# Cutting VectorE's long steps of an attention-and-experts block into pieces with places of their own

## The reference

```python
x = x + layernorm(attention(layernorm(x)))
x = x + layernorm(experts(layernorm(x)))
# attention: 16 heads of 16 channels, rotary q and k, causal, softmax, W_o
Q, K, V = (split_heads(layernorm(x) @ W.T) for W in (W_q, W_k, W_v)); Q, K = rope(Q), rope(K)
out = softmax(where(causal, -inf, Q @ K.T / 4)) @ V @ W_o.T
# experts: 16 of 128 hidden channels, 4 chosen for each token, and a shared one of 256
scores = sigmoid(h @ gate_w.T); groups of 4, the best 2 of 4 groups, then the best 4 experts of these
y = sum over chosen e of w_e * (silu(h @ Wg[e].T) * (h @ Wu[e].T)) @ Wd[e].T
y = y + (silu(h @ Ws_g.T) * (h @ Ws_u.T)) @ Ws_d.T ;  return h + y      # all float32
```

## Time and profile before

| | |
|---|---|
| Time, median of 3 runs | 1130.15 us (1129.67 to 1133.27) |
| The profiled execution's own time | 1136.02 us |
| Its span | 1134.2 us |
| TensorE busy | 886.7 us (78%) |
| VectorE busy | 679.0 us (60%) |
| ScalarE, GpSimd busy | 448.6 us (40%), 440.0 us (39%) |
| Mean granted TensorE clock | 0.844 of 2.4 GHz |

### The profile page before, as it was taken

The page is one execution under the profiler, slowest core; times in us unless marked ns, Lnnn a source line. Parts: engine busy times, 40 slices in busy tenths (PEclk is TensorE's granted clock), DMA queues, the critical chain, the costliest instruction groups (busy, mean ns, idle before and its releaser), DMA issues.

```text
span 1134.2 us, 21559 instructions
## 1 busy us (share of the span) xinstructions
PE 886.7 (78%) x7044; PEld 651.4 (57%) x7044; DVE 679.0 (60%) x1918; ACT 448.6 (40%) x756; POOL 440.0 (39%) x422
## 2 busy tenths in 40 slices
PE   4369798887987997888886798695987699988810
PEld 3245465664654665655564555584875588877700
DVE  4467658677668578577476475552652233677737
ACT  2115444444343444443442445342542355444400
POOL 4422113125316316306313114454555545555642
PEclk9659898897798698798696789898998999988955
DMA  3684716217226235324465322343544555987764
GB/s 131 149 228 106 215 39 168 67 36 216 73 53 176 85 76 163 103 76 115 118 228 178 106 73 93 112 149 105 158 138 159 169 164 166 362 303 260 243 243 149
DMA packets 101467, 168.78 MB, mean 149 GB/s; under 512 B 14704, under 2 KB 73072, under 8 KB 101104
## 3 DMA queue, kind: packets, MB, share of 16 engines
q1 hardware_dynamic: 87536, 128.85, 39.7%
q0 software_dynamic: 13824, 38.55, 9.0%
HBM read 90.15 MB, written 76.68 MB: 147 GB/s over the span
## 4 chain that ended last, share of the span: by engine, by line
PE 46%; DVE 17%; issue 11%; SPq 8%; DMA 7%; ACT 6%; POOL 3%; another core or an unknown queue 2%; ACTq 0%; DVEq 0%; POOLq 0%
PE ring L1444 6%; PE ring L1316 6%; PE ring L1250 5%; PE ring L1251 4%; PE ring L1252 4%; PE ring L1287 4%; PE ring L1302 4%; ACT prob L1180 3%; DVE nmax L778 3%; DMA xg<-sorted_rows 3%; PE ring L1465 3%; SPq L581 2%; PE ring L1264 2%; PE ring L1430 2%
## 5 line engine op out<-in xcount | busy, mean ns | idle before, releaser
L778 DVE TENSOR_REDUCE nmax<-ring 128x2 f32<-128x1024 f32 (+3 forms) x256 | 201.2, 818 | 103.8 <-PE ring L1293 87.3
L1180 ACT ACTIVATE prob<-ring 128x1024 f32<-128x1024 f32 (+1 forms) x192 | 164.1, 879 | 217.4 <-PE ring L1307 195.8
L688 POOL DMA_INDIRECT expert_rows<-ys,dest x160 | 157.1, 982 | 139.3 <-ACT ys L1134 80.5
L680 POOL DMA_INDIRECT sorted_rows<-xr,idx_all x128 | 127.5, 996 | 86.9 <-DVE xr L937 53.7
L1444 PE MATMUL ring<-we,xh 128*128 x640 | 159.8, 395 | 0.0
L1287 PE MATMUL ring<-k_st,q_st 48*128 48x512 f32 (+3 forms) x512 | 116.0, 460 | 42.4 <-ACT prob L1180 35.6
L1302 PE MATMUL ring<-q_st,k_st 50*128 50x384 f32 (+3 forms) x512 | 109.3, 445 | 34.0 <-DMA q_st<-mrow 10.8
L1444 PEld LDWEIGHTS ring<-we,xh 128*128 128x128 f32 x640 | 121.6, 200 | 14.4
L1000 DVE SCALAR_TENSOR_TENSOR sl<-sl,got,ring 128x128 f32<-128x128 f32 x160 | 48.4, 344 | 123.1 <-ACT sl L1232 88.3
L1316 PE MATMUL ring<-prob,v_sb 128*32 128x512 f32 (+3 forms) x1024 | 111.6, 539 | 0.8 <-ACT prob L1180 0.4
L658 POOL TENSOR_TENSOR rot<-rot 128x512 f32<-128x512 f32 x16 | 20.4, 1273 | 222.5 <-DVE rot L770 222.5
(11 more groups left out here) (192 smaller groups left out, 1672.3 us busy)
## 6 DMA issues: line engine op xcount, KB each, us to landing
xg<-sorted_rows SPq DMA_DIRECT2D x160, 134.0 KB
parts<-part SPq DMA_DIRECT2D x32, 512.0 KB
ykt<-expert_rows SPq DMA_DIRECT2D x16, 1024.0 KB
k_st<-parts SPq DMA_DIRECT2D x64, 128.0 KB
q_st<-parts SPq DMA_DIRECT2D x64, 128.0 KB
we<-w_exp SPq DMA_DIRECT2D x1, 6144.0 KB, 20.0
sorted_rows<-zeros SPq DMA_DIRECT2D x2, 2144.0 KB, 10.5
sorted_rows<-zeros SPq DMA_DIRECT2D x32, 134.0 KB
```

Of the source, the lines that this page charges most:

```text
L680: pool.indirect_dma_start(out=xs[group_of(s)], out_offset=bass.IndirectOffsetOnAxis(ap=idx_all[:, s, t, k:k + 1], axis=0), in_=xr[:, s % 2 ...
L688: pool.indirect_dma_start(out=yk, out_offset=bass.IndirectOffsetOnAxis(ap=dest[:, j % 8, b:b + 1], axis=0), in_=ys[:, j % NYS, b, :], in_o ...
L778: dve.tensor_reduce(nmax[:, Q % 2, :, pp, qb], slot[:, :, col:col + (qb + 1) * P], AX.X, ALU.max, negate=True).then_inc(s_max, 1)
L1180: act_e.activation(prob[:, u % 2, 2 * half:2 * half + 2, 0:width], slot[:, :, 0:width], ACT.Exp, scale=SCALE).then_inc(s_exp, 1)
```

## The change

Nine kinds of step of VectorE are no longer done at one place of the list but in pieces, each with a time of its own: `LN` in three (two bn_stats, two bn_stats, the rest), `LNR` in two, the rotary step in two (`QK`: the even half, `QKB`: the odd half), `LNA` in three, `LNB` in seven, `LNC` in two, `Z` in two, `DP` and `GE` in four. The residual sum of `LNB` becomes two sums of two tiles each. Every other engine keeps its steps; where such a step is a part of a split kind (GpSimd's power, its rotary sums, SP's stores), it now stands at the place of the piece named in the diff. The scatters move from 34.5 + 0.55n to 34.7 + 0.54n.

```diff
-AFTER = [("X1L", 18), ("AT", 22), ("OP", 23), ("LNA", 24), ("LNB", 25), ("LNC", 26), ("HT", 27),
+AFTER = [("X1L", 18), ("AT", 22), ("OP", 23), ("HT", 27),
...
-AFTER += [("SD", 30.5), ("Z", 30.501), ("CNT", 33.5), ("DP", 33.9)]
+AFTER += [("LNB", i, (24.55, 24.75, 25.0, 25.3, 25.55, 25.75, 26.0)[i]) for i in range(7)]
+AFTER += [("SD", 30.5), ("Z", 0, 30.501), ("Z", 1, 30.65), ("CNT", 33.5)]
...
-N_LN = 5 * NT + 1
+N_LN = 5 * NT + 2
...
@@ gpsimd
-                elif kind == "QK":
+                elif kind == "QKB":
                     rotate(n, st[2])
...
-                elif kind in ("LNA", "LNB"):
-                    post_rstd(n, int(kind == "LNB"))
+                elif kind == "LNA" and st[2] == 2:
+                    post_rstd(n, 0)
+                elif kind == "LNB" and st[2] == 6:
+                    post_rstd(n, 1)
@@ vector
+            def rotary(s, qk, slot, second):
...
+                if not second:
...
+                    dve.wait_ge(s_qk, 4 * s + 2 * qk + 1)
+                    dve.tensor_tensor(rot[:, 0, :], even, cos, ALU.mult).then_inc(s_rot, 1)
+                    dve.tensor_tensor(rot[:, 2, :], even, sin, ALU.mult).then_inc(s_rot, 1)
+                    return
                 dve.wait_ge(s_qk, 4 * s + 2 * qk + 2)
...
+            def residual(s, i):
                 done = N_LN * s + 2 * NT
+                if i < 2:
+                    dve.wait_ge(s_lnr, 2 * s + 1)
+                    for t in (2 * i, 2 * i + 1):
+                        dve.tensor_scalar(pr[:, t, :], pr[:, t, :], mv2[:, t, 0:1], rstd2[:, t:t + 1],
+                                          ALU.subtract, ALU.mult).then_inc(s_ln, 1)
+                elif i < 4:
+                    h = slice(2 * (i - 2), 2 * (i - 1))
+                    dve.wait_ge(s_x1in, 16 * (s + 1))
+                    dve.wait_ge(s_ln, done + 2 * (i - 1))
+                    dve.tensor_tensor(x1[:, h, :], x1[:, h, :], pr[:, h, :], ALU.add).then_inc(s_ln, 1)
+                else:
+                    dve.wait_ge(s_ln, done + NT + 2)
+                    statistics(x1, s_ln, done + NT + 2, i - 4)
...
                 elif kind == "Z":
-                    if n:
+                    a = st[2]
+                    if n and a == 0:
                         dve.wait_ge(s_zst, 16 * n)
-                    for a in range(NHALF):
...
```

## The result

The changed kernel takes 1138.87 us (median of 17 runs, 1134.06 to 1150.03) against 1130.15 (17 runs), a ratio of **1.0072 (1.0048 to 1.0095)**: slower by 8.7 us, where 8.6 were forecast. In two later measurements, on two chips, it was 1.0105 (1.0064 to 1.0147) and 1.0132 (1.0098 to 1.0165). So the sign held each time, and the size in this one. The parts of the sum did not hold as well, as the experiments show.

A forecast was written before the change was run, and what follows sets the result against it. TensorE, busy 78%, bounds it, many VectorE steps ending just in time. Z 5.2, first rotary 3.7, second rotary with norms 2.6, table -6.9, last sequence 4: +8.6 us on 1130.15, so 1139 us, range 1122 to 1150.

The forecast's parts named there:

- `Z`, 5.2 us: At the split sum Z, a maximum before the second half makes ST wait, at six places: +5.2 us.
- so 0.9 us are left as a loss: At Z, ST comes 1.5 us later, partly offset at the next S, leaving 0.9 us lost per just-in-time place.
- The rotary steps, 3.7 and 7.4: At the first and second rotary step, odd products stand behind other work, so TensorE waits: +3.7 and +7.4 us.
- The norms, -4.8: Behind the second rotary step, the split norms shorten TensorE's waits for maxima and before HT: -4.8 us.
- the wait for the power: Before LNC, VectorE newly waits for GpSimd's power, being idle for 1 to 2 us.
- rival (c): At the norms, GpSimd's subtractions stall LNB's residual sums instead of LNC: +12 us, 1151 us; chance 12%.
- The subtractions are ready about when the sums end: At the norms, the argument that GpSimd's subtractions would hardly meet LNB's residual sums, against a stall of 2.5 us per sequence.
- The table, -6.9: At DP, GE and GR, mainly in the fifth sequence, split pieces shorten TensorE's waits: -6.9 us, of it -1.1 at GR.
- a clock of a sequence that moves by over 0.05: For any sequence, a sign that the forecast is wrong: its clock moves by over 0.05.
- The last sequence, +4: In the last sequence, GpSimd's second power stands behind seven more scatters, delaying LNC and expert gating: +4 us (0 to 8).
- all 18 places: Six places each at Z, the first and the second rotary step, where TensorE was to wait for VectorE.

The follow-up runs named there:

- rot_together: The changed kernel with the odd half of both rotary steps right behind the even half again: 1110.15 us, 1.0386 of the kernel before.
- z_rot_together: The changed kernel with both halves of Z together and both rotary steps whole again: 1094.59 us, 1.0255 of the kernel before.
- rotary_z_alone: Against the kernel before, only both rotary steps and Z split, norms, DP and GE whole: 1145.02 us, 1.0166.
- norms_alone: Against the kernel before, only LN, LNR, LNA, LNB and LNC split, rotary steps, Z, DP and GE whole: 1122.07 us, 1.0000.
- tables_alone: Against the kernel before, only DP and GE split, with the scatters moved and the residual sum in two halves: 1119.89 us, 0.9987.
- tail_whole: The changed kernel with LNA, LNB and LNC whole at their old places in the last sequence only: 1098.78 us, 1.0262 of the kernel before.
- part_after_rows: The kernel before, with GpSimd's subtractions of the second rotary step made to wait until LNC has written its rows: 1125.14 us, 0.9970.

## Why the prediction was right, and where its steps were not

**`Z`, 5.2 us.** The wait is there, in all six places, 8.0 us more in all (1.6 before, 9.6 after; over the three profiles of each 2.7 and 9.0, so 6.3 more). The step that failed is the netting, "so 0.9 us are left as a loss". Nothing is given back at the next `S`: in the steady sequence of `rot_together` against `z_rot_together` the wait for `z` is 1.4 us and those for exponentials are 1.5 longer instead of shorter. The price there was 15.6 us. Part of it is the clock: from the sixth to the seventh `Z` it is 0.81 against 0.97, and the stretch takes 64.0 against 55.7 us. What `Z` costs on the chip of the forecast was not measured by itself.

**The rotary steps, 3.7 and 7.4.** TensorE's wait for them is 15.3 us, as forecast (15). As a price it is wrong on chip A: with `Z` whole, splitting them cost 0.2 us, where the sum had 3.7 + 7.4 = 11.1, or 6.3 if the norms' return of 4.8 goes with it. The wait took the place of waits for maxima that follow in the same stretch, and the clock gave back the rest. With `Z` split only the estimate above speaks, and with whole norms it was not tried; `rotary_z_alone` gives only the sum of both parts, 18.8 against 16.3.

**The norms, -4.8.** Their net was right on its chip (1.000 with the last sequence, where the sum had -4.8 + 4; the parts of the -4.8 add up to 4.6), `LNC` and the wait for the power (1.16) were right, but the mechanism was that of rival (c), to which I gave 12%: the subtraction did issue before a residual sum, in four sequences, 2.2 us each. "The subtractions are ready about when the sums end" was the wrong step. They did not cost 12, as TensorE's wait of 1.93 became one of 1.46 and one of 1.80, and its other wait, 1.47 before `HT`, went from this sequence. The stall in `pr` was in no term. Nor was the loss at the first sequence's norms, where the sum had a return of 1.4 us and `norms_alone` falls behind by 2.7; a better clock in `norms_alone` (24.0 against 32.8 us at the lower level) covers it there. So the net came out by things that cancel.

**The table, -6.9.** The stretch from the fifth to the sixth `Z` is shorter by just that, the wait at `GR` by 3.3 us, not 1. But alone the part gave 1.5 us, and its stretch is 3.7 us shorter (86.6), while `norms_alone`, with a whole table, has the same short stretch as after (82.9). So the agreement is no proof of the term. The next stretch is longer, mostly through the clock. Windows of these two stretches, before (second profile), then after:

```profile
568.30:658.80 90.50, 69.77 (x652) 47.22 (x653) 54.08 (x146) 33.94 (x48) 20.34 (x20) 0.75 0.54 172
658.80:714.40 55.60, 47.42 (x528) 31.76 (x528) 35.21 (x108) 32.10 (x45) 19.01 (x18) 0.97 0.18 62
```

```profile
580.70:663.50 82.80, 69.33 (x685) 46.58 (x684) 53.97 (x146) 34.77 (x49) 20.68 (x20) 0.81 0.62 188
663.50:724.00 60.50, 50.40 (x514) 32.91 (x509) 35.35 (x111) 32.51 (x45) 18.34 (x18) 0.86 0.17 57
```

Before, TensorE runs the second stretch at 0.97; in after at 0.86, and works 3 us longer for the same matmuls. This is not the table's gain given back: `tables_alone` has a shorter first stretch and runs the second at 0.97 (54.4 us), `rotary_z_alone` has no gain in the first (91.5) and runs the second at 0.78 (61.6). What lets the clock fall there is open. It is one of the signs by which I wanted to know a wrong forecast, a clock of a sequence that moves by over 0.05, and it came. The Trainium skill ("TensorE: Matmul & The Clock Gate", section "HAM oscillation — how this bites in real kernels") has idle gaps cost again through the clock. Here the rows show both signs: after has 2.9 us more idle time in a sequence and no lower clock (31.6 against 32.8 us at 1.2 GHz), and `norms_alone` and `tables_alone` have more idle time than before and the best clock of all (24.0).

**The last sequence, +4.** The power does move: it starts 17.5 us after the first one instead of 9.4, 8.1 more, as the scatters had it (seven more stand ahead of it; two of them, both `expert_rows`, stand ahead of the first power too). `tail_whole` puts its price at 8.2, the upper bound, on chip A. In the change as a whole, in the three measurements off that chip, that stretch is only 0.6 us longer. There before has a wait of 11.35 us for `sl` at 780.40 (9.19 in its second profile), which after has not. It is gone in `norms_alone` and in `rotary_z_alone` as well, and stands in `tables_alone` (9.73) and `part_after_rows` (11.22); what frees it is open.

**The total.** 8.6 came true as 8.7 by the medians (8.1 by the ratio), and as 11.8 and 14.9 by the ratio in the two later measurements. The sign rests on the just-in-time steps of the earlier trace rows, which were read rightly: the waits came at all 18 places, about as long as forecast. The exact number is luck: `Z` was priced too low, the rotary steps and the table too high, the loss at the first sequence's norms and that of the clock behind the sixth `Z` were in no term, and on another chip the same working would have missed by 3 or 6 us, on chip A by some 30, by the estimate above.

## What to carry to other kernels

What is put ahead of a step that ends just in time for the busy engine becomes a wait of that engine, and its length can be read from the trace beforehand. Its price can't: here waits of about the same length cost 15.6 us at `Z` and 0.2 at the rotary steps, by what waited behind them and by the clock. A split that moves a two-input or `tensor_scalar` step of VectorE must be laid against GpSimd's list: the cut norms won nothing here (1.0000), as the pieces met its operations, while one wait on GpSimd (`part_after_rows`) won 3.4 us. Measure parts alone and together, on one chip: here norms and tables cost nothing one by one on one chip and 27 us together on another.

## What the runs showed of the hardware

- VectorE's `tensor_tensor` and `tensor_scalar` from SBUF to SBUF wait for the end of a GpSimd `tensor_tensor` of 128x512: also a `tensor_scalar` of 128x4 (0.17 to 0.65 us) and one with a single wide input (0.41 to 0.77). `bn_stats` (0.43 both times) and the two that read PSUM (0.69 both times) do not. GpSimd's power of 128x2 (0.80 us), a `tensor_tensor` too, did not hold one up: a `tensor_scalar` of 128x256 begun 0.15 us behind it (1103.01 us in after) took 0.41 us. The Trainium skill ("SBUF — State Buffer", section "Summary: rules for kernel authors") says it of a VectorE operation with two SBUF inputs or in 2-port mode; the trace agrees (0.69 to 1.20 with two inputs).
- The same program took 1067.67, 1120.91, 1129.85 and 1130.15 us on the chips of four measurements. Only ratios within one chip compare, and the ratio moved too, from 1.0072 to 1.0132.
- Kernels with more idle time of TensorE can be faster: `norms_alone` has 13.1 us of it in a sequence, before 11.6, and is 2.8 us shorter there, with 24.0 against 32.8 us at the lower clock (one execution against the mean of three).
